# Bilinear sampling as two multiply-adds and a scale, and a last stage in 16-row units with four landing slots

## The reference

```
x  = x + deform_conv(_gn(x))
g  = _gn(x)
h1 = relu(batchnorm(conv3x3(g, ternary(w1))))
h2 = batchnorm(conv3x3(h1, ternary(w2)))
out = x + relu(h1 + h2)

# deform_conv: om = conv3x3(x, w_off) + b_off has 27 channels: 9 offsets (y, x) and 9 masks
g(y0, x0, hy*hx) + g(y0, x0+1, hy*lx) + g(y0+1, x0, ly*hx) + g(y0+1, x0+1, ly*lx)   # bilinear, hy = 1-ly, hx = 1-lx
sampled = sampled * sigmoid(mask)
out = einsum('bckhw,ock->bohw', sampled, w_conv)      # k: the 9 taps
```

## Time and profile before

| | |
|---|---|
| median of 3 runs | 3130.37 us |
| the profiled execution | 3130.63 us |
| its span, first to last instruction | 3129.0 us |
| PE busy | 2624.7 us (84%) |
| DVE busy | 2243.4 us (72%) |
| ACT busy | 1207.7 us (39%) |
| POOL busy | 1331.4 us (43%) |
| mean granted clock of PE | 0.926 |
| DMA | 827.53 MB, mean 264 GB/s |

### The profile page before, as it was taken

How to read it: one execution, slowest core, us unless ns; L and a number is a source line. 1 busy time by engine, 2 the same in 40 slices (tenths; PEclk the granted TensorE clock), 3 DMA queues, 4 the chain that set the end, 5 groups by cost and what they waited for, 6 DMA issues and landing times. The chain is left out here.

```text
span 3129.0 us, 40030 instructions
## 1 busy us (share of the span) xinstructions
PE 2624.7 (84%) x11674; PEld 1748.8 (56%) x11674; DVE 2243.4 (72%) x6010; ACT 1207.7 (39%) x2103; POOL 1331.4 (43%) x1294
## 2 busy tenths in 40 slices
PE   4768888888999999899899999998998969999500
PEld 2434444445655566565565555555555769999500
DVE  5478888888878878888788878778875246666544
ACT  1234343444444444544344444434442123323244
POOL 1045555554554555445455555555550013333111
PEclk9788999999999999999999999999999989999755
DMA  5579999998999998989899998999993211111387
GB/s 158 175 265 343 346 335 337 336 355 290 329 334 334 347 341 321 320 301 337 295 330 333 332 320 314 330 325 336 326 323 119 70 55 57 57 49 58 114 278 252
DMA packets 286852, 827.53 MB, mean 264 GB/s; under 512 B 26204, under 2 KB 59996, under 8 KB 285924
## 3 DMA queue, kind: packets, MB, share of 16 engines
q0 software_dynamic: 170496, 620.83, 55.0%
q1 hardware_dynamic: 116196, 204.94, 19.9%
HBM read 740.19 MB, written 85.48 MB: 264 GB/s over the span
## 5 line engine op out<-in xcount | busy, mean ns | idle before, releaser
L360 POOL DMA_INDIRECT G<-pixel_pairs,quad_c x1152 | 1145.8, 995 | 1009.6 <-PE psT L783 724.7
L646 DVE SCALAR_TENSOR_TENSOR G<-G,wts_c 128x256 f32<-128x256 f32 x3456 | 1407.3, 480 | 211.5 <-ACT G L408 203.8
L746 PE MATMUL psD<-ST,wconv 128*128 128x512 f32 x2304 | 1073.3, 612 | 0.0
L746 PEld LDWEIGHTS psD<-ST,wconv 128*128 128x128 f32 x2304 | 436.3, 199 | 455.2 <-issue 455.2
L735 PE MATMUL psF<-pf,qw 128*128 128x512 f32 x2304 | 631.5, 423 | 14.6 <-DVE pf L570 7.6
L408 ACT ACTIVATE G<-G,wts_c 128x256 f32<-128x256 f32 x1152 | 507.5, 500 | 190.9 <-DMA G<-pixel_pairs,quad_c 153.5
L735 PEld LDWEIGHTS psF<-pf,qw 128*128 128x128 f32 x2304 | 429.3, 189 | 163.6 <-issue 54.7
L783 PE MATMUL psT<-idn,G 128*128 128x128 f32 x2304 | 326.8, 288 | 188.4 <-DVE G L646 188.4
L445 ACT ACTIVATE ST<-psT 128x1024 f32<-128x1024 f32 x288 | 293.7, 1020 | 437.4 <-PE psT L783 437.3
L783 PEld LDWEIGHTS psT<-idn,G 128*128 128x128 f32 x2304 | 279.3, 148 | 267.8 <-issue 133.4
L735 PE MATMUL psA<-po,woff 128*64 128x512 f32 x1152 | 349.8, 452 | 6.3 <-DVE po L570 6.3
(11 more groups left out here) (137 smaller groups left out, 1652.6 us busy)
## 6 DMA issues: line engine op xcount, KB each, us to landing
pixel_pairs<-yT SPq DMA_DIRECT2D x112, 256.0 KB, 5.3
G<-pixel_pairs,quad_c POOLq DMA_INDIRECT x1152, 6.3
xz<-in_x SPq DMA_DIRECT2D x32, 512.0 KB, 6.1
xres<-in_x SPq DMA_DIRECT2D x32, 512.0 KB, 7.1
x<-x1c SPq DMA_DIRECT2D x32, 512.0 KB
h<-h1c SPq DMA_DIRECT2D x32, 512.0 KB, 3.9
area<-h SPq DMA_DIRECT2D x32, 512.0 KB, 6.8
area<-x SPq DMA_DIRECT2D x32, 512.0 KB, 5.3
```

The source lines that it names most:

```text
L360: pool.indirect_dma_start(out=G[:, i % RING, :], out_offset=None, in_=tbl[d.b].rearrange("y x q c -> (y x) (q c)"), in_offset=bass.Indirec ...
L646: dve.scalar_tensor_tensor(g[:, 0:C], g[:, q * C:(q + 1) * C], wts_c[:, d.p, q * NG + i:q * NG + i + 1], g[:, 0:C], ALU.mult, ALU.add).the ...
L746: ins = pe.matmul(psD[:, oc, :], wconv[:, t, k, oc * 128:(oc + 1) * 128], ST[:, k % 3, t, :], start=(k == 0 and t == 0), stop=(k == TAPS - ...
```

## The change

The three multiply-adds and the scaling of one gathered row become two multiply-adds and a scaling. With lx / hx and ly / hy as weights, the first multiply-add takes both corners at x0+1 (512 columns) times lx / hx and adds them to the two at x0; the second takes 256 columns times ly / hy; ACT then multiplies by mask * hy * hx. So ACT comes behind DVE and before PE. DVE now waits for the gathers, ACT for the second multiply-add, PE for ACT's scaling (d_scaled). In ACT's order of a step the copy to ST of tap k - 1 now stands before the scaling of tap k. The block's weights are three and not four, and `indices` takes a maximum and a reciprocal for the division.

The last stage works in 16 units of 16 rows. h1 and x1 of a unit land in one of four slots. The slots lie in SBUF that the convolution used: `area`, the buffers pg, and the weights in po and qw; so unit 0 is loaded when the last block has been split, and units 1 to 3 once PE has finished. relu1 writes to PSUM. All stores are issued by SP, in the same loop as the loads: the loads of unit n + 4, then the store of unit n.

```
 
                 def emit(s, z, o, d, f, o2, f2):
                     for k in range(TAPS):
+                        if d and k > 0:
+                            st_evac(d, k - 1)
                         if d:
                             if k == 0:
                                 act.wait_ge(d_pick, d.n + 1)
                             for t in range(PT):
                                 i = PT * k + t
-                                act.wait_ge(d_g[i % RING], 16 * (NG // RING * d.n + i // RING + 1))
+                                act.wait_ge(d_mac, 2 * NG * d.n + 2 * PT * k + PT + t + 1 + CREDIT)
                                 g = G[:, i % RING, 0:C]
-                                act.activation(g, g, ACT.Copy, scale=wts_c[:, d.p, i:i + 1]).then_inc(d_m0, 1)
+                                act.activation(g, g, ACT.Copy, scale=wts_c[:, d.p, i:i + 1]).then_inc(d_scaled, 1)
                         if f and f.first and k == (2 if d else 1):
                             group_sqrt((1, f.b))
                         if z and z.last and k == 6:
                             group_sqrt((0, z.b))
-                        if d and k > 0:
-                            st_evac(d, k - 1)
                         if o and 1 <= k < 1 + PT:
                             act.wait_ge(o_tr, PT * o.n + k + CREDIT)
...
-                    w4 = wts[:, ds(o.r, 1), :].rearrange("p r (q i) -> p (r q) i", q=4)
+                    w3 = wts[:, ds(o.r, 1), :].rearrange("p r (q i) -> p (r q) i", q=3)
                     m9 = mk[:, 0, :].rearrange("p (t k) -> p k t", t=PT)
                     go(dve.tensor_tensor(kt(mk[:, 1, :]), m9, yx(P, 0), ALU.mult))
-                    go(dve.tensor_tensor(kt(mk[:, 2, :]), m9, yx(Lf, 0), ALU.mult))
-                    for q in range(4):
-                        ins = dve.tensor_tensor(kt(w4[:, q, :]), kt(mk[:, 1 + q % 2, :]), yx((P, Lf)[q // 2], 1), ALU.mult)
+                    go(dve.tensor_tensor(kt(w3[:, 0, :]), kt(mk[:, 1, :]), yx(P, 1), ALU.mult))
+                    go(dve.tensor_scalar(P, P, 2.0 ** -25, None, ALU.max))
+                    go(dve.reciprocal(P, P))
+                    for q in range(2):
+                        ins = dve.tensor_tensor(kt(w3[:, 1 + q, :]), yx(P, 1 - q), yx(Lf, 1 - q), ALU.mult)
                     go(ins)
...
-                        need(dve, d_mac, 3 * NG * (d.n - 1) + CREDIT)
-                        need(dve, d_m0, NG * (d.n - 1) + CREDIT)
+                        need(dve, d_mac, 2 * NG * (d.n - 1) + CREDIT)
+                        need(dve, d_scaled, NG * (d.n - 1) + CREDIT)
                         dve.tensor_copy(wts_c[:, d.p, :], wts[:, ds(d.r, 1), :].rearrange("p r i -> p (r i)")).then_inc(d_pick, 1)
                         dve.wait_ge(d_pick, d.n + 1)
                     if s == NB and f.is_row(5):
                         weight_extremes(1)
                     for k in range(TAPS):
                         if d:
-                            for q in range(1, 4):
+                            for q, w in ((1, 2 * C), (2, C)):
                                 for t in range(PT):
                                     i = PT * k + t
                                     g = G[:, i % RING, :]
                                     if q == 1:
-                                        dve.wait_ge(d_m0, NG * d.n + i + 1 + CREDIT)
+                                        dve.wait_ge(d_g[i % RING], 16 * (NG // RING * d.n + i // RING + 1))
                                     else:
-                                        dve.wait_ge(d_mac, 3 * NG * d.n + 3 * PT * k + PT * (q - 2) + t + 1 + CREDIT)
-                                    dve.scalar_tensor_tensor(g[:, 0:C], g[:, q * C:(q + 1) * C], wts_c[:, d.p, q * NG + i:q * NG + i + 1],
-                                                             g[:, 0:C], ALU.mult, ALU.add).then_inc(d_mac, 1)
-                                dve.memset(pause[:, 3 * k + q - 1:3 * k + q], 0.0)
+                                        dve.wait_ge(d_mac, 2 * NG * d.n + 2 * PT * k + t + 1 + CREDIT)
+                                    dve.scalar_tensor_tensor(g[:, 0:w], g[:, w:2 * w], wts_c[:, d.p, q * NG + i:q * NG + i + 1],
+                                                             g[:, 0:w], ALU.mult, ALU.add).then_inc(d_mac, 1)
...
-                            need(pe, d_mac, 3 * NG * d.n + 3 * PT * (k + 1) + CREDIT)
+                            need(pe, d_scaled, NG * d.n + PT * (k + 1) + CREDIT)
...
-            h1w, x1w = (area[:, i * CT * PX:(i + 2) * CT * PX].rearrange("p (s x) -> p s x", s=2) for i in (0, 2))
...
+            EU, ESLOTS = 2 * PX, 4
+            NEU = NCH * PX // EU
+
+            own_flat = own[:].rearrange("p n r w -> p (n r w)").bitcast(F32)
+            po_f, qw_f = po_flat.bitcast(F32), qw[:].rearrange("p t k o -> p (t k o)").bitcast(F32)
+            land = [[r[:, i * CT * EU:(i + 1) * CT * EU].rearrange("p (t x) -> p t x", t=CT) for r in (area, own_flat, po_f, qw_f)]
+                    for i in range(2)]
...
+            ps_r1 = psG[:].rearrange("p q t j x -> p q t (j x)")
...
-                hold(sp, g_split, NCH + CR)
-
-                with sp.Fori(0, NCH // NR) as j:
-                    for u in range(NR):
-                        b, r = j, u
-                        hold(sp, e_mac, NR * j + u - 1 + CR)
-                        sp.dma_start(h1w[:, u % 2, :].rearrange("p (t x) -> p t x", t=CT), rows_of(h1_d, b, r * RC, RC)).then_inc(e_lh[u % 2], 16)
-                        hold(sp, e_sum, NR * j + u - 1 + CR)
-                        sp.dma_start(x1w[:, u % 2, :].rearrange("p (t x) -> p t x", t=CT), rows_of(x1_d, b, r * RC, RC)).then_inc(e_lx[u % 2], 16)
+
+                def store_out(j, v):
+                    hold(sp, e_sum, ESLOTS * j + v + 1 + ESLOTS)
+                    sp.dma_start(rows_of(out, j, v * (EU // W), EU // W), h2[:, :, ds((ESLOTS * j + v) * EU, EU)]).then_inc(e_st, 16)
+
+                def load_unit(j, v):
+                    hold(sp, e_r1, CT * (ESLOTS * j + v - ESLOTS + 1) + CT * ESLOTS)
+                    sp.dma_start(h1w[v], rows_of(h1_d, j, v * (EU // W), EU // W)).then_inc(e_lh[v], 16)
+                    hold(sp, e_sum, ESLOTS * j + v - ESLOTS + 1 + ESLOTS)
+                    sp.dma_start(x1w[v], rows_of(x1_d, j, v * (EU // W), EU // W)).then_inc(e_lx[v], 16)
+
+                sp.sem_inc(e_r1, CT * ESLOTS)
+                sp.sem_inc(e_sum, ESLOTS)
+                sp.wait_ge(g_split, NCH + CR)
+                load_unit(0, 0)
+                sp.wait_ge(g_conv, NCH + CR)
+                for v in range(1, ESLOTS):
+                    load_unit(0, v)
+                with sp.Fori(0, NEU // ESLOTS - 1) as j:
+                    for v in range(ESLOTS):
+                        load_unit(j + 1, v)
+                        store_out(j, v)
+                for v in range(ESLOTS):
+                    store_out(NEU // ESLOTS - 1, v)
+                sp.wait_ge(e_st, 16 * NEU)
...
-                with act.Fori(0, NCH // NR) as j:
-                    def relu1(u):
-                        act.wait_ge(e_lh[u % 2], 16 * (NR // 2 * j + u // 2 + 1))
+                with act.Fori(0, NEU // ESLOTS) as j:
+                    def relu1(v):
+                        act.wait_ge(e_lh[v], 16 * (j + 1))
+                        act.wait_ge(e_mac, ESLOTS * j + v - 1 + CR)
                         for t in range(CT):
-                            v = h1w[:, u % 2, t * PX:(t + 1) * PX]
-                            act.activation(v, v, ACT.Relu, bias=bias_b[:, 0, t:t + 1], scale=scale_b[:, 0, t:t + 1]).then_inc(e_r1, 1)
-
-                    def relu2(u):
-                        act.wait_ge(e_mac, NR * j + u + 1 + CR)
+                            act.activation(ps_r1[:, v % 2, t], h1w[v][:, t], ACT.Relu,
+                                           bias=bias_b[:, 0, t:t + 1], scale=scale_b[:, 0, t:t + 1]).then_inc(e_r1, 1)
+
+                    def relu2(v):
+                        act.wait_ge(e_mac, ESLOTS * j + v + 1 + CR)
                         for t in range(CT):
-                            v = h2[:, t, ds((NR * j + u) * PX, PX)]
-                            i = act.activation(v, v, ACT.Relu, bias=bias_b[:, 1, t:t + 1], scale=1.0)
+                            h = h2[:, t, ds((ESLOTS * j + v) * EU, EU)]
+                            i = act.activation(h, h, ACT.Relu, bias=bias_b[:, 1, t:t + 1], scale=1.0)
                         i.then_inc(e_r2, 1)
                     relu1(0)
-                    for u in range(1, NR):
-                        relu1(u)
-                        relu2(u - 1)
-                    relu2(NR - 1)
+                    for v in range(1, ESLOTS):
+                        relu1(v)
+                        relu2(v - 1)
+                    relu2(ESLOTS - 1)
...
-                    def mix(u):
+                with dve.Fori(0, NEU // ESLOTS) as j:
+                    def mix(v):
                         for t in range(CT):
```

(59 more changed lines are left out.)

3 lines of the change are left out of this document (2 added, 1 removed).

## The result

The changed kernel takes 3020.26 us (median of 4 runs, 3015.74 to 3026.24), the kernel before beside it on the same chip 3130.62 (4 runs, 3129.79 to 3131.74): ratio 0.9648, 95% interval 0.9628 to 0.9669. The prediction was 3048, with 3018 to 3090 as its range: the direction and the main mechanisms hold, the gain is 110 us and not 82. The median lies only 2 us inside that range, and under the 3031 to 3065 that the prediction gave the forecast itself.

What follows compares the result with a forecast made beforehand. PE was taken to bound the middle 16 blocks, with DMA near its limit in the outer ones. 3130.6 - 26 (deformable stage) - 56 (last stage) = 3048.6, median 3048; own range 3031 to 3065, 8 of 10 in 3018 to 3090.

Steps and rivals of the forecast that it cites:

- DVE's work per tap: Deformable stage: a tap's multiply-adds on DVE take 4.3 us instead of 4.82, some 150 us less over 288 taps.
- The first stretch, 20 us: First 8 blocks (197 to 718 us): PE waits less for taps 5 and 8, 2.1 + 0.43 us a block, 20 us.
- T(1), 0.43 us: PE's transposes of tap 1, all 32 blocks: 0.43 us sooner, as DVE is free when psD ends.
- T(4) in the third stretch, 0.5 us late: PE's transposes of tap 4, last 8 blocks (1852:2370): 0.5 us late, since tap 3's scaling precedes ACT's normalising of next rows.
- The last stage, 56 us: After PE's end: DMA full at 365 GB/s, loads from 2934.5 us, end at 3073 instead of 3129, 56 us less.
- 1 (nothing from the deformable stage): The deformable stage gains nothing: 3074 us, to 3082 if tap 4's transposes are late in 24 blocks; chance 0.2.
- 2 (60 us from DVE running ahead): Deformable stage: DVE starts on gathers as they land and PE's clock no longer dips, 60 us less: 3015; chance 0.13.
- 3: Last stage not full of DMA, 258 to 300 GB/s, only 11 to 30 us less: 3076 to 3095; chance 0.1.
- 4: ACT becomes the last hand before every transpose, PE losing 0.5 us at each of 288 taps: 3218 us; chance 0.05.

Runs made afterwards that it cites:

- finish_later: Changed kernel with DVE's x1c and bn_stats of the block before moved behind tap 1's multiply-adds: 2961.82 us, ratio 0.9476.
- norm_first: Changed kernel with ACT normalising the next rows between the copy to ST and the scaling, not behind the scaling: 3019.48 us, ratio 0.9655.
- two_slots: Changed kernel with two slots instead of four for the last stage's units of 16 rows: 3061.23 us in one run.
- no_early: Changed kernel with units 1 to 3 loaded only when the batch norm of h2 is known, not at PE's end: 3030.14 us, ratio 0.9698.
- sampling_only: Changed first program (new sampling) with the last stage of the kernel before: 3099.77 us, ratio 0.9918.
- copy_after: Changed kernel with ACT's old order, scaling of tap k first and copy to ST of tap k - 1 behind it: 3089.90 us, ratio 0.9879.

## Why the prediction was right, and where its sizes were off

- **DVE's work per tap.** Right. The 512-column operation takes 749 ns (taken: 751), and a whole tap 4.25 us (2159.40 to 2163.65), taken 4.3. (The tap of before is 4.88 us by the two times that the prediction names, not 4.82.) Over all taps the multiply-adds fell from 1407.3 us to 808.8 + 481.5 = 1290.3, 117 less where I had 150.
- **The first stretch, 20 us.** 25 measured (19 to 25 over the runs), blocks of 62.1 us where I had 62.6. That it comes so near is partly luck. Right: T(5)'s wait is gone, and gathers are late next. Wrong: T(1) gave nothing here (0.43 us a block in the sum), and T(7)'s wait, which the sum does not have, grew by 1.2 us a block: PE is there sooner, the last gather is not (T(7) started 4.3 to 5.5 us behind it before, 3.0 now). Left out: PE's busy time fell by 11.7 us, nearly half of the gain; T(5) took 1.76 us in the earlier trace rows and takes 1.04 now. I laid what stays to the gathers alone. T(1)'s chain was 26 us of it, which finish_later took away; T(7)'s wait is the gathers', though half the bytes win only 13 us.
- **T(1), 0.43 us.** 0.47 in the block shown. It holds in most blocks of the middle and the third stretch, where x1c had begun late, and in none of the first: at most 24 blocks and not 32. The middle's 9.3 us are not this alone: 5.6 of them arise in one block, where T(0) waited 7.9 us before and 2.9 after. The step saw the chain but not what it offers: nearly three quarters of T(1)'s wait (3.2 of 4.4 us) went when x1c and bn_stats no longer stood ahead of tap 1.
- **T(4) in the third stretch, 0.5 us late.** T(4) comes 6.48 us after T(3), where the step before it took 6.21: 0.27 late, with no wait marked on the row. Over the eight blocks the mean wait at T(4) went from 0.1 to 0.5 us, and most of it is block 25, where T(4) waits 2.6 us and the block takes 71.7 us, before 68.0. To psG the stretch is 3.1 us longer where I had 1 less; over the runs with the same first program it is 0.2 to 3.1 longer. norm_first takes 701.4 us from block 25 to psG, less than all of these (704.5 to 707.4), with block 25 at 70.7; that fits its expected 3 us, and is too little to show in its time. The cause of block 25's loss stays open.
- **The last stage, 56 us.** The mis-sized term of the sum. The mechanism is right (depth keeps DMA full, an earlier start: two_slots and no_early), with about 7 MB in flight and not 3, but the rate was 418 GB/s in the middle of the stage (402 over all of it) and not 365. I had chosen between 350 and 413 nearer to the lower one. With 418 the same sum gives 2904.3 + 1.4 + 115.4 + 5 = 3026, within 2 us of what came (3024.2). The 0.37 us of SP for an issue was too low as well: in the full queue it is 1.6 to 2.8 us, and DMA stayed full all the same. The Trainium skill ("DMA: Bandwidth & Descriptors", Bandwidth, Measured) has 425 GB/s for large loads; this stream of loads and stores reaches 417 to 421 in its windows from 2930 to 3020 us, so the trace agrees within 2%. (The 358 GB/s of its "HBM Reference" stand there under Specifications (TRN2), not under Access.) The estimate made with it was 19 us earlier than mine; the stage was 18.6 us shorter than the 138.5 forecast.
- **Rivals.** 1 (nothing from the deformable stage) fell to sampling_only: 0.9918, upper end 0.9938. 2 (60 us from DVE running ahead) did not occur in that way; a gain of that size was there, but behind DVE's order. 3 fell: share 1.0; it is what two_slots shows (309 GB/s). 4 did not happen, but a loss through ACT was near: copy_after, with ACT's old order, loses 70 us. The move of the copy, which avoids that, is in the change, but the prediction gives it no term.

## What to carry to other kernels

When an operation changes sides (from before another engine to behind it), price its neighbours' order on its own engine as a term of its own: here that one move was worth 70 us, more than the whole gain of 30. Where a transfer stage is to be filled, keep transfers queued and take the rate from the fullest row of the trace, not from the mean of packets that stood in gaps. A mean DMA share tells little of one late gather: look how long before the awaited instruction it landed. And look at each wait for the instructions ahead of it that nobody waits for: moving them past the awaited ones gave 58 us with one changed number.

## What the runs showed of the hardware that was not expected

- One queue of SP carried 48.24 MB in 120 us, loads and stores mixed, at a share of 1.00:

```profile
q1 hardware_dynamic: 12512, 48.24, 99.8%
...
out<-h SPq DMA_DIRECT2D x16, 1024.0 KB, 17.5
```

A store of 1 MB lands 17.5 us after its issue there, in two_slots after 8.7. By an estimate from the rate (17.5 us x 418 GB/s = 7.3 MB) some seven transfers are in flight. In the full queue an issue holds SP itself for 1.6 to 2.8 us (2934 to 2998 us), against 0.37 to 0.5 where the queue has room:

```profile
2922.51 0.40 SPq L896 DMA_DIRECT2D out<-h  x1
...
2951.22 1.92 SPq L896 DMA_DIRECT2D out<-h  x1
```
- Rows of 2 KB in transfers of half the size cost 4% against rows of 4 KB at a full DMA (404 and 419 GB/s).
- PE's granted clock in the third stretch, a mean over the stretch, rose from 0.95 to 0.98 in finish_later, when the waits at T(1) were shorter. After 4.41 us of waiting T(1) took 1.97 us in the changed kernel, after 1.21 us of waiting 1.09 here. PE's busy time fell by 10 us with it (477.10 us for the 1738 matrix instructions of 1819:2340 in the changed kernel, 467.44 for 1743 here), beside the idle time saved:

```profile
1764.50:2275.00 510.50, 467.44 (x1743) 281.08 (x1741) 368.70 (x818) 214.66 (x386) 292.58 (x287) 0.98 0.90 325
```
